# A graph attention block on one core: the first microseconds reordered, small loads later, and half of x asked for by a second queue

## What is computed

```python
h = jnp.maximum(_layernorm(x, axis=-1), 0.0)          # x: 384 x 1024, float32
q = h @ wq.T + bq ; k = h @ wk.T + bk ; v = h @ wv.T + bv          # 1024 x 1024 weights
q2 = (q @ wiq.T + biq).reshape(N, H, D).transpose(1, 0, 2)         # H = 16 heads of D = 64
k2 = (k @ wik.T + bik)...  ; v2 = (v @ wiv.T + biv)...
mask = full((N, N), -inf).at[src, dst].set(w[edge_type - 1])       # 6528 edges, last one wins
scores = einsum('hnd,hmd->hnm', q2, k2) / 8 + mask
out = einsum('hnm,hmd->hnd', softmax(scores), v2)
return x + out.reshape(N, 1024) @ wo.T + bo
```

## Time and profile before

| | us |
|---|---|
| median of three runs | 304.92 |
| the profiled execution | 304.59 |
| its span, first to last instruction | 302.8 |
| TensorE matmul busy (share of the span) | 295.2 (98%) |
| TensorE weight loads busy | 270.4 (89%) |
| VectorE busy | 179.8 (59%) |
| ScalarE busy | 153.4 (51%) |
| GpSimd busy | 149.3 (49%) |
| TensorE's share of the chain that ended last | 91% |

### The profile page before, as it was taken

One profiled execution on the slowest core, in us unless ns is written; L12 is line 12 of the kernel. 1 busy time (PEld: TensorE's weight loads), 2 busy tenths in 40 slices (PEclk: granted clock), 3 DMA queues, 4 the chain that ended last, 5 costly groups with the idle time before them and its releaser, 6 DMA issues.

```text
span 302.8 us, 4742 instructions
## 1 busy us (share of the span) xinstructions
PE 295.2 (98%) x1707; PEld 270.4 (89%) x1707; DVE 179.8 (59%) x475; ACT 153.4 (51%) x288; POOL 149.3 (49%) x152
## 2 busy tenths in 40 slices
PE   6899999999999999999999999999999999999996
PEld 3689998888899999999999999999999998787886
DVE  3889978784544444344487756566665656647241
ACT  1886433252533344433345684949494949874100
POOL 5431544643465454555101993938383848964000
PEclk9999999999999999999999999999999999999999
DMA  6978875739533334443733133030313121400031
GB/s 187 391 207 257 276 229 197 215 127 349 207 139 107 111 133 139 139 132 103 252 105 124 28 125 128 8 135 16 124 28 114 55 85 65 146 0 2 0 139 69
DMA packets 15817, 40.82 MB, mean 135 GB/s; under 512 B 3481, under 2 KB 4914, under 8 KB 15794
## 3 DMA queue, kind: packets, MB, share of 16 engines
q1 hardware_dynamic: 13490, 39.29, 38.8%
q0 software_dynamic: 2016, 1.21, 1.6%
q10 hardware_dynamic: 288, 0.03, 0.1%
HBM read 37.71 MB, written 2.81 MB: 134 GB/s over the span
## 4 chain that ended last, share of the span: by engine, by line
PE 91%; DVE 3%; ACT 2%; DMA 1%; POOL 1%; issue 1%; SPq 0%
PE bank L805 26%; PE bank L809 25%; PE bank L806 25%; PE bank L923 5%; PE bank L908 4%; PE bank L938 3%; PE bank L939 3%; DMA x_sb<-in_x 1%; DVE a_lo L661 1%; DVE stats L633 1%; POOL rstd L347 1%; DVE prob L724 0%; PE bank L857 0%; ACT pt_hi L510 0%; ACT work L517 0%
## 5 line engine op out<-in xcount | busy, mean ns | idle before, releaser
L388 POOL DMA_INDIRECT cells<-value,cell x51 | 55.6, 1090 | 57.4 <-DMA cells<-value,cell 46.0
L805 PE MATMUL bank<-a_hi,w_hi 128*128 128x384 f32 x192 | 64.7, 337 | 0.0
L809 PE MATMUL bank<-a_lo,w_hi 128*128 128x384 f32 x192 | 64.4, 335 | 0.0
L806 PE MATMUL bank<-a_hi,w_lo 128*128 128x384 f32 x192 | 64.2, 334 | 0.0
L427 ACT ACTIVATE w_hi<-raw 128x1024 fp32r<-128x1024 f32 x51 | 54.0, 1058 | 19.1 <-PE bank L809 17.3
L668 DVE TENSOR_TENSOR w_lo<-raw,w_hi 128x1024 fp32r<-128x1024 f32 x36 | 44.0, 1223 | 15.2 <-ACT w_hi L427 14.6
L406 POOL TENSOR_SCALAR prob<-prob,row_inv 128x384 f32<-128x384 f32 x36 | 23.0, 646 | 41.5 <-DVE row_inv L734 41.5
L361 POOL TENSOR_TENSOR w_lo<-raw,w_hi 128x1024 fp32r<-128x1024 f32 x15 | 36.0, 2397 | 8.7 <-ACT w_hi L427 8.7
L805 PEld LDWEIGHTS bank<-a_hi,w_hi 128*128 128x128 f32 x192 | 36.0, 188 | 1.0 <-POOL w_lo L361 0.3
L809 PEld LDWEIGHTS bank<-a_lo,w_hi 128*128 128x128 f32 x192 | 36.0, 188 | 0.4 <-DVE a_lo L681 0.4
L806 PEld LDWEIGHTS bank<-a_hi,w_lo 128*128 128x128 f32 x192 | 36.1, 188 | 0.0
(11 more groups left out here) (135 smaller groups left out, 608.4 us busy)
## 6 DMA issues: line engine op xcount, KB each, us to landing
raw<-in_slabs SPq DMA_DIRECT2D x56, 512.0 KB
x_sb<-in_x SPq DMA_DIRECT2D x6, 256.0 KB, 4.8
work<-key_rows SPq DMA_DIRECT2D x6, 256.0 KB, 4.6
prob<-key_rows SPq DMA_DIRECT2D x6, 256.0 KB, 3.8
x_sb<-in_x SPq DMA_DIRECT2D x3, 512.0 KB, 5.8
out_y<-x_sb SPq DMA_DIRECT2D x5, 256.0 KB, 2.1
cells<-prob SPq DMA_DIRECT2D x2, 576.0 KB, 8.9
cells<-value,cell POOLq DMA_INDIRECT x51
```

Source lines behind the costliest of these rows:

```text
L388: nc.gpsimd.indirect_dma_start(out=cells[c][:, :], out_offset=bass.IndirectOffsetOnAxis(ap=cell[:, t:t + 1], axis=0), in_=value[:, t:t + 1 ...
L805: nc.tensor.matmul(psum, w[0], a[0], start=first, stop=False)
L806: nc.tensor.matmul(psum, w[1], a[0], start=False, stop=False)
L809: return nc.tensor.matmul(psum, w[0], a[1], start=False, stop=last)
```

## The change

It rewrites the beginning; everything after the first tiles keeps its work, with shifted places of three queues.

- x's right halves are issued by ScalarE's queue, left ones by SyncE's. `ew` and `bias` move from ScalarE's queue to SyncE's, behind slab 1, and the edge tables behind them.
- The right half of the last tile: VectorE computes max(x - mean, 0) before the last shift, then multiplies by rstd. ScalarE's last relu is cut into two pieces of 256 columns.
- w_hi of slab 0, right half: VectorE (a cast) instead of ScalarE. w_lo of slab 0, both halves: GpSimd. The left half of it was VectorE's.
- GpSimd's key row comes after w_lo of slab 1. SyncE's wait for it stands behind slab 3, and all key loads move one slab later.
- `UNIT_ORDER` swaps each pair of units, and the first scatter no longer waits for all edge values.
- TensorE: no warm products after the last tile's transposes; in the first tile the transposes of the right half stand between the second and third product.

```diff
-WARM = [18, 4, 3, 2]
+WARM = [18, 4, 3]
-UNIT_ORDER = [0, 6, 1, 7, 2, 8, 3, 9, 4, 10, 5, 11, 12]
+UNIT_ORDER = [6, 0, 7, 1, 8, 2, 9, 3, 10, 4, 11, 5, 12]
...
             for t in range(NT):
-                for b in range(2):
-                    half = slice(b * HALF, (b + 1) * HALF)
-                    sp_eng.dma_start(x_sb[:, t, half], x[t * P:(t + 1) * P, half]).then_inc(x_in[t][b], 16)
+                sp_eng.dma_start(x_sb[:, t, 0:HALF], x[t * P:(t + 1) * P, 0:HALF]).then_inc(x_in[t][0], 16)
...
-                if s == 0:
+                if s == 1:
+                    sp_eng.dma_start(ew[:], edge_weights.rearrange("(a n) -> a n", a=1).to_broadcast([P, 4])).then_inc(
+                        ew_in, 16)
+                    sp_eng.dma_start(bias[:], biases).then_inc(small_in, 16)
                     for i in range(2):
...
+                if s == 3:
                     sp_eng.wait_ge(key_row_ok, 1)
                     sp_eng.dma_start(key_rows[0, :].rearrange("(t e) -> t e", e=P), key_row[:]).then_inc(keys_out, 16)
-                if 3 <= s < 3 + GROUPS:
-                    if s == 3:
+                if 4 <= s < 4 + GROUPS:
+                    if s == 4:
                         sp_eng.wait_ge(keys_out, 16)
...
-            half = slice(HALF, F)
-            pool.wait_ge(slab_hi, 1)
-            nc.gpsimd.tensor_tensor(w_lo[:, 0, half], raw[:, 0, half], w_hi[:, 0, half].bitcast(F32),
-                                    ALU.subtract).then_inc(slab_lo, 1)
+            pool.wait_ge(shift_ok, NT)
+            for b in range(2):
+                half = slice(b * HALF, (b + 1) * HALF)
+                pool.wait_ge((half_hi, early_hi)[b], 1)
+                nc.gpsimd.tensor_tensor(w_lo[:, 0, half], raw[:, 0, half], w_hi[:, 0, half].bitcast(F32),
+                                        ALU.subtract).then_inc((half_lo, slab_lo)[b], 1)
...
-                    pool.wait_ge(value_ok, 1)
+                    pool.wait_ge(sp_ok, 1)
...
-            act.dma_start(ew[:], edge_weights.rearrange("(a n) -> a n", a=1).to_broadcast([P, 4])).then_inc(ew_in, 16)
-            act.dma_start(bias[:], biases).then_inc(small_in, 16)
+            for t in range(NT):
+                act.dma_start(x_sb[:, t, HALF:F], x[t * P:(t + 1) * P, HALF:F]).then_inc(x_in[t][1], 16)
...
-                part = slice(0, F) if t < NT - 1 else slice(0, HALF)
+                for part in [slice(0, F)] if t < NT - 1 else [slice(b * HALF // 2, (b + 1) * HALF // 2) for b in range(2)]:
...
-                if k == 1:
-                    first_slab_hi(1)
-                if k == 4:
+                if k == KT // 2:
                     split_hi(1)
...
+            h_last = x_sb[:, NT - 1, HALF:F]
+            nc.vector.tensor_scalar(h_last, h_last, mean_var[:, NT - 1, 0:1], 0.0, ALU.subtract,
+                                    ALU.max).then_inc(h_step, 1)
             shift_part(NT - 1)
-            nc.vector.tensor_scalar(h_last, h_last, rstd[:, NT - 1:NT], shift[:, NT - 1:NT], ALU.mult,
-                                    ALU.add).then_inc(h_step, 1)
             dve.wait_ge(h_step, 1)
-            nc.vector.tensor_scalar(h_last, h_last, 0.0, None, ALU.max).then_inc(h_last_ok, 1)
-            half = slice(0, HALF)
-            dve.wait_ge(half_hi, 1)
-            nc.vector.tensor_tensor(w_lo[:, 0, half], raw[:, 0, half], w_hi[:, 0, half].bitcast(F32),
-                                    ALU.subtract).then_inc(half_lo, 1)
+            nc.vector.tensor_scalar(h_last, h_last, rstd[:, NT - 1:NT], None, ALU.mult).then_inc(h_last_ok, 1)
+            dve.wait_ge(slab_in[0], 16)
+            nc.vector.tensor_copy(w_hi[:, 0, HALF:F], raw[:, 0, HALF:F]).then_inc(early_hi, 1)
...
+            def first_tile():
...
+                pe.wait_ge(half_lo, 1)
+                for k in range(KT):
+                    c = slice(k * P, (k + 1) * P)
+                    if k == KT // 2:
+                        wait_lo(pe, 0)
+                    pe.wait_ge(h_hi, k + 1)
+                    nc.tensor.matmul(psum[:, 0:N], hi[:, c], a_hi[:, k, :], start=(k == 0), stop=False)
+                    nc.tensor.matmul(psum[:, 0:N], lo[:, c], a_hi[:, k, :], start=False, stop=False)
+                    if k == 0:
+                        pe.wait_ge(h_last_ok, 1)
+                        for late in range(KT // 2, KT - 1):
+                            turn_h(late, NT - 1)
+                    pe.wait_ge(h_lo, k + 1)
+                    mm = nc.tensor.matmul(psum[:, 0:N], hi[:, c], a_lo[:, k, :], start=False, stop=(k == KT - 1))
```

More of the change, by code:

```diff
@@ L392, in _ @@
             split_lo(1)
+            pool.wait_ge(rows_in, 32)
+            nc.gpsimd.tensor_copy(rows[:], rows_i[:]).then_inc(rows_ok, 1)
+            pool.wait_ge(rows_ok, 1)
+            nc.gpsimd.tensor_scalar(key_row[:], rows[:, 0, :], float(N), 0.0, ALU.mult, ALU.add).then_inc(rows_ok, 1)
+            pool.wait_ge(rows_ok, 2)
+            nc.gpsimd.tensor_tensor(key_row[:], key_row[:], rows[:, 1, :], ALU.add).then_inc(key_row_ok, 1)
             done = 0
@@ L815, in tile @@
             def tile(t, a_h, a_l, ks=range(KT)):
-                if t == 0 and ks[-1] < KT // 2:
-                    pe.wait_ge(half_lo, 1)
-                    hi, lo = split_place(0)
-                else:
-                    hi, lo = split_slab(slab_of(t))
+                hi, lo = split_slab(slab_of(t))
                 if t > 3 * KT + 4:
@@ L830, in tile @@
                     mm = products(psum[:, 0:N], (hi[:, c], lo[:, c]), (a_h[:, k, :], a_l[:, k, :]), k == 0,
[L831 removed]
+                                  k == KT - 1)
                 if k == KT - 1:
```

58 lines of the change are left out of this document (25 added, 33 removed).

## The result

The changed kernel is slower: 307.25 us median of 20 runs (304.98 to 309.47), beside 304.48 for the kernel before (20 runs, 304.25 to 305.57); ratio 1.0083, 95% interval 1.0065 to 1.0101. The forecast was 304.5, its range up to 305.9. The profiled execution took 307.35 us, span 305.4. The changed kernel was not taken again in those batches, so a difference from its 307.25 is one between batches, and a few tenths of it are not resolved.

The account below looks back on a forecast made before the run. TensorE was taken as the bound (98% busy), with VectorE second, without slack at 27.07. Terms: 0.3 (x) + 0.2 (beginning, behind VectorE) - 0.1 (keys) = 0.4 us, from median 304.92 to 304.5; range 303.3 to 305.9.

Parts of the forecast that it names:

- x: Loading x through two queues, small loads moved away: gain 0.3 us, bounds 1.1 gain and 0.7 loss.
- cap: Limit on x's gain: fifth half lands with the sixth, at 8.9 less 0.5, so tile 2 gains 0.2.
- upper bound of 1.1: Best case for x: both first halves land at 3.8, second statistics start at 4.5, gaining 1.1.
- rival 1: x really comes early because small loads had slowed its first halves: x gains 1.1, total 303.7; chance 0.20.
- The beginning: Work up to TensorE's tile 1: shorter last shift, earlier splits of slabs 0 and 1; tile 1 starts 0.54 earlier.
- the 0.68: GpSimd's w_lo of slab 1 ends at 18.06 instead of 18.74, because ScalarE's w_hi starts earlier.
- VectorE behind it: VectorE after tile 1's start, held by GpSimd's key-row work: loses 0.5, so 0.2 of the 0.54 survives.
- The keys: First key load on SyncE's queue, behind the later key row: VectorE waits 0.1, bounds 0 and 1.5.
- Slab 4 ... costs nothing: Slab 4 asked for 0.7 to 1.9 later on SyncE; its products come after tile 3, so no cost.
- Rival 2: Keys come late: VectorE stands 1.5 us, delaying tile 1's b_lo and tile 3; 305.9, chance 0.17.
- Mask and scatter: New unit order starts the second scatter chain after the first unit; mask comes earlier, nothing on the path.

Follow-up runs that it names:

- e4: Kernel before with only x's right halves asked for by ScalarE's queue, ahead of the two small loads: 303.60 us, ratio 0.9967.
- e1: Changed kernel with GpSimd's key row worked out between the low parts of slab 0 and that of slab 1: 303.83 us, ratio 0.9979.
- e3: Changed kernel with 12 throwaway products on TensorE between tiles 2 and 3: 305.92 us, ratio 1.0037.
- e7: Changed kernel with SyncE asking for slab 4 ahead of its wait for the key row and the row's write: 305.14 us, ratio 1.0027.
- e11: Changed kernel with VectorE taking tile 1's low part ahead of the first unit of keys: 306.75 us, ratio 1.0069.
- e6: Kernel before with only the key row moved behind slab 1's low part, keys loaded from slab 4 on: 307.92 us, ratio 1.0121.
- e2: Changed kernel with all six halves of x asked for by SyncE, as before: 307.69 us, ratio 1.0113.
- e10: Changed kernel with edge rows behind x's left halves, key row before the last pow, and slab 1 waiting for x's last tile: 305.21 us, ratio 1.0037.
- e12: Changed kernel with edge rows behind x's left halves, key row before the last pow, small loads behind slab 0, tile 1's low part before keys: 303.16 us.

## Why the prediction was wrong

**x: wrong size, too small.** The term was 0.3, with a cap: "with halves in pairs, the fifth lands with the sixth". Alone it is 0.9 (e4), near its own upper bound of 1.1 and rival 1's 303.7. The cap was a landing time of one crowded queue (5.8 us after the issue, rows 7), read as if it were the transfer's own; the 0.5 taken off it for the small loads came from no row. In the changed kernel's profiled execution the cap seems to hold: tile 2's first half comes at 8.36 with a wait of 0.78, a gain of 0.2. But e1, e3, e7 and e11 ask for the same loads up to there and took it up at 7.64 to 7.88, and the old order gives 8.57 and, in e6, 8.28. So the same edit is worth between nothing and 0.9 at this place, from one execution to the next; what decides that is open. By its profile the gain did not need the second queue (e2). The Trainium skill's rule ("DMA: Bandwidth & Descriptors", Issuing engines are not separate DMA queues) is that a second queue saves only issue time, and e2's profile agrees with it; I had drawn from it that the term is near zero, and left out that the edit also takes the small loads from in front of x.

**The beginning: right.** Shift 0.16 long; pow 0.72 instead of 0.55, a loss of 0.17 where I took 0.10; VectorE's cast of w_hi held by GpSimd's w_lo (11.45, 1.50 long), as described. The third product came at 13.50, forecast 14.05 less x's share; w_lo of slab 1 ended at 17.65, forecast 18.06 less 0.3 for x; tile 1 gained 1.06, where the two terms gave 0.54 + 0.3. Two slips in the working changed nothing: 14.05 + 0.5 + 21 x 0.17 is 18.12, not 18.25, and the 0.68 counts 0.08 between ScalarE's end and GpSimd's start that was not saved (0.61).

**VectorE behind it: right in kind, too large in size.** I took 0.5 lost to GpSimd. A 4-column instruction is again stretched to 0.70 beside GpSimd (16.98), and the key row's middle instruction takes 1.22 beside VectorE's w_lo. GpSimd's low part ended 1.09 earlier than before and VectorE was 0.9 earlier at the keys, so 0.2 was lost and the gain survived up to there.

**The keys: the step that failed.** "I take a wait of 0.1; bounds 0 and 1.5" is where the forecast breaks. The times ahead of it were right: the row ready at 19.86 (19.4 or 20.6 forecast), its write 1.65 (2.1). The load was not: 4.54 us, where I allowed 2.5 to 3.5 and argued that "the queue is emptier at 20 us than it was at 16.8". (The 2.5 was an estimate that no run bears out; the shortest first load in the 14 traces is 3.5.) The queue isn't emptier: slab 4 is asked for 1.4 us ahead of the load and slab 5 0.4 behind it; e7, with slab 4 away, gives 3.49, the figure of rows 7, though e10 and e12, alike in this, give 4.3 and 4.2. And the load was needed at 24.06, not 24.75, since x and the beginning brought VectorE there sooner. Wait: 26.18 - 24.06 = 2.12 where the sum had 0.1, and all of it reached TensorE. The fall of the clock behind it is in no term of the sum and in no rival.

**"Slab 4 ... costs nothing": wrong.** Its own products did not wait, as I argued; but its transfer ran beside the load that was urgent, and with the row late that made about 2.1 us (e7), most of it through the clock. I asked when slab 4 is needed, and not whose transfer it meets.

**Rival 2: the right mechanism, priced too low.** It named every link (row, write, load, VectorE, b_lo, tile 3) and the point of decision, "later than 25.2"; the load landed at 26.1. Its 305.9 left out the clock: a stall of that length is followed by products 0.32 apart in most runs, 1.3 us (e3). That 305.9 and 1.3 come to the measured 307.25 is partly luck: the wait was 0.6 longer than its 1.5, the gain ahead of it 0.6 larger than its 0.5, and the median it starts from, 304.92, was 0.4 higher than that of 20 runs. Its chance, 0.17, rested on an emptier queue that the row of no transfer supported.

**Mask and scatter: right.** TensorE has no gap after tile 4 that it did not have before, and no wait for the mask.

## What to carry to other kernels

When an edit moves a wait on a queue, ask of each transfer behind it not only when its own data is needed but which urgent transfer it will now run beside; here a 512 KB slab asked for 1.4 us ahead of an urgent load, in a queue that was also busy behind it, cost about 2.1 us, the clock's share included (e7). It mattered only because the load was already late (e1). A rearrangement that frees an engine early brings forward the time at which that engine needs its next input, so a load that was just in time becomes late by the gain. And a stall of about 2 us on TensorE is to be priced above its length: in this kernel the clock fell behind it in most executions and cost 1.3 us more by the median.
